# On VectorE, one of four h tiles turned; orders of a two-layer graph kernel made anew; the last z begins as h in three tiles

## What is computed

```python
def reference(x, adj, bias, W_lang, W_grav, W_V, W_O, gate_logit, log_sigma):
    h = layernorm(x + einsum('bnf,nm->bmf', x, adj * adj) + bias)       # layer 0
    z_l, z_g = h @ W_lang.T, h @ W_grav.T                               # layer 1
    v = h @ W_V.T
    zn = z_l / max(norm(z_l), EPS)
    A_l = max(zn @ zn.T, 0) * not_eye
    d2 = max(sq + sq.T - 2 * z_g @ z_g.T, 0)                            # sq = sum(z_g**2)
    A_g = exp(-d2 / (2 * sigma**2)) * not_eye
    K_l, K_g = (A * adj / max(sum(A * adj), EPS) for A in (A_l, A_g))
    K = w * K_l + (1 - w) * K_g                                         # w = sigmoid(gate)
    return layernorm(h + (K @ v) @ W_O.T)
```

## Time and profile before

| | us |
|---|---|
| median of 3 runs | 587.3 (585.48 to 588.52) |
| the profiled execution, timed | 588.2 |
| its span in the profile | 586.2 |

### The profile page before, as it was taken

How to read it: one execution, slowest core, us unless ns; L and a number is a source line. 1 busy time by engine, 2 the same in 40 slices (tenths; PEclk the granted TensorE clock), 3 DMA queues, 4 the chain that set the end, 5 groups by cost and what they waited for, 6 DMA issues and landing times.

```text
span 586.2 us, 9873 instructions
## 1 busy us (share of the span) xinstructions
PE 573.7 (98%) x3653; PEld 445.0 (76%) x3653; DVE 422.2 (72%) x956; ACT 293.5 (50%) x516; POOL 128.0 (22%) x344
## 2 busy tenths in 40 slices
PE   8999999999999999999999999999999999999993
PEld 6887868687786868688686868778686868868771
DVE  4943785858688685858779585868868585877584
ACT  4644536365553546465463636555354646535341
POOL 0201113132222303122221313222230312222021
PEclk9999999999999999999999999999999999999997
DMA  8813031321313031131303112131313110100011
GB/s 273 212 39 72 1 73 32 72 61 55 91 51 76 37 99 29 54 91 56 89 29 98 38 63 65 54 91 44 82 37 94 35 55 18 55 18 22 33 73 72
DMA packets 20783, 38.67 MB, mean 66 GB/s; under 512 B 2176, under 2 KB 2176, under 8 KB 20736
## 3 DMA queue, kind: packets, MB, share of 16 engines
q1 hardware_dynamic: 20736, 38.05, 23.0%
HBM read 21.27 MB, written 16.78 MB: 65 GB/s over the span
## 4 chain that ended last, share of the span: by engine, by line
PE 95%; DVE 2%; DMA 1%; issue 0%; POOL 0%; SPq 0%; ACT 0%; POOLq 0%; DVEq 0%
PE ring L389 65%; PE bank_s L408 10%; PE bank_y L349 3%; PE bank_z L430 3%; PE bank_y L430 2%; PE bank_z L362 2%; PE bank_y L362 2%; PE bank_s L349 2%; PE ring L480 2%; PE ring L503 1%; DMA yT<-in_L_gnn_W_lang_dram 1%; PE bank_s L480 1%; PE bank_y L415 0%; PE bank_s L503 0%; PE ring L473 0%
## 5 line engine op out<-in xcount | busy, mean ns | idle before, releaser
L567 ACT ACTIVATE yT<-ring 128x512 f32<-128x512 f32 x128 | 73.0, 595 | 153.1 <-PE ring L389 153.1
L389 PE MATMUL ring<-hT_hi,T_hi 128*128 128x512 f32 x320 | 126.3, 395 | 0.0
L389 PE MATMUL ring<-hT_hi,T_lo 128*128 128x512 f32 x320 | 124.5, 389 | 0.0
L389 PE MATMUL ring<-hT_lo,T_hi 128*128 128x512 f32 x288 | 112.2, 390 | 0.0
L389 PE MATMUL ring<-M_hi,hT_hi 128*128 128x512 f32 x256 | 102.9, 402 | 0.0
L773 DVE TENSOR_TENSOR hT_lo<-hT,hT_hi 128x512 fp32r<-128x512 f32 x64 | 42.3, 682 | 80.0 <-ACT hT L567 79.6
L389 PE MATMUL ring<-M_lo,hT_hi 128*128 128x512 f32 x256 | 100.0, 390 | 0.0
L389 PE MATMUL ring<-M_hi,hT_lo 128*128 128x512 f32 x256 | 99.9, 390 | 0.0
L389 PEld LDWEIGHTS ring<-hT_hi,T_hi 128*128 128x128 f32 x320 | 60.1, 188 | 25.1 <-issue 12.2
L609 ACT ACTIVATE h_sb<-h_sb,z_nb,z_rs 128x512 f32<-128x512 f32 x62 | 50.3, 813 | 43.2 <-POOL z_nb L1095 43.2
L389 PEld LDWEIGHTS ring<-hT_hi,T_lo 128*128 128x128 f32 x320 | 60.1, 188 | 12.6
(11 more groups left out here) (141 smaller groups left out, 821.3 us busy)
## 6 DMA issues: line engine op xcount, KB each, us to landing
x_sb<-in_x_dram SPq DMA_DIRECT2D x32, 512.0 KB, 6.5
out_dram<-h_sb SPq DMA_DIRECT2D x60, 256.0 KB, 2.0
yT<-in_L_gnn_W_lang_dram SPq DMA_DIRECT2D x4, 256.0 KB, 3.6
yT<-in_L_gnn_W_grav_dram SPq DMA_DIRECT2D x1, 1024.0 KB, 7.3
h_sb<-in_L_gnn_W_V_dram SPq DMA_DIRECT2D x1, 1024.0 KB, 11.8
h_sb<-in_L_gnn_W_O_dram SPq DMA_DIRECT2D x1, 1024.0 KB, 12.7
out_dram<-h_sb SPq DMA_DIRECT2D x8, 128.0 KB, 2.3
bias_bc<-in_L_gnn_bias_dram SPq DMA_DIRECT2D x1, 256.0 KB, 9.0
```

The source lines that it names most:

```text
L389: last = pe.matmul(ring[ring_of(g, k)][:, :], a, b, start=n == 0, stop=n == len(terms) - 1)
L567: return act.activation(dst, src, ACT.Copy, scale=scale)
```

## The change

1. From group 1 on the last of the four h tiles (p = 3) is turned by VectorE, in the new function `turn_h`. Its first instruction turns the 32x32 blocks of the whole tile in place, each in its own 32 partitions, straight from `h_sb` into `hT`; twelve more, of 32 partitions by 128 elements, then write the blocks whose partitions differ. ScalarE makes `hT_hi` of this tile from `hT` in SBUF, and makes no `hT` copy. The new semaphores are `hT_turned_own` and `hT_turned`; `copied` counts the three tiles a group that are still turned by TensorE.
2. The orders of `step` are new on TensorE, ScalarE, VectorE and GpSimd. TensorE does both halves of layer 0, then both of apply_k; one transposed tile goes ahead of the gram, and two behind projection 9.
3. In the last group `residual` is done for tiles 1, 2 and 3, ahead of `apply_k(g, 0)`; tile 1 is counted from PSUM and loses its addition on VectorE.

The core of the diff (of the orders a few lines):

```diff
+            def turn_h(g):
+                dve.wait_ge(h_ready, NP * g + NP)
+                B = N // 2
+                to = hT_view(hT[g % 2], NP - 1).rearrange("f i c (q b) -> f i c q b", q=2)
+                rows_h = h_sb[g % 3][:, NP - 1, :].rearrange("r (i k b) -> r i k b", i=DC, k=4)
+                dve.transpose(hT_view(hT[g % 2], NP - 1),
+                              h_sb[g % 3][:, NP - 1, :].rearrange("r (i c n) -> r i c n", i=DC, c=2)).then_inc(
+                                  hT_turned_own, 1)
+                dve.wait_ge(hT_turned_own, g)
+                for k in range(4):
+                    for q in range(4):
+                        if k != q:
+                            last = dve.transpose(to[k * B:(k + 1) * B, :, q // 2, q % 2, :],
+                                                 rows_h[q * B:(q + 1) * B, :, k, :])
+                last.then_inc(hT_turned, 1)
...
             def hi_hT(g, p):
-                act.wait_ge(hT_done, NP * g + p + 1)
+                if g > 0 and p == NP - 1:
+                    act.wait_ge(hT_turned, g)
+                    copy(hT_view(hT_hi[g % 2], p), hT_view(hT[g % 2], p)).then_inc(hT_hi_done, 1)
+                    return
+                act.wait_ge(hT_done, copied(g, p))
...
@@ TensorE, step
                 layer0(g + 1, 0)
+                layer0(g + 1, 1)
                 if tail:
                     apply_k(g - 1, 0)
-                layer0(g + 1, 1)
-                if tail:
                     apply_k(g - 1, 1)
...
                 transpose_h(g + 1, 0)
-                transpose_h(g + 1, 1)
                 gram(g)
                 project(g, 9)
+                transpose_h(g + 1, 1)
                 transpose_h(g + 1, 2)
-                transpose_h(g + 1, 3)
...
@@ TensorE, last group
-            apply_k(g, 0)
+            residual(g, 1)
             residual(g, 2)
             residual(g, 3)
+            apply_k(g, 0)
             apply_k(g, 1)
...
@@ ScalarE, step
-                evict(g, 6)
                 normalise_h(g + 1, 0)
                 normalise_h(g + 1, 1)
+                normalise_h(g + 1, 2)
+                evict(g, 6)
+                normalise_h(g + 1, 3)
                 evict(g, 7)
...
@@ VectorE, last group
             add_z(g, 0)
-            add_z(g, 1)
+            count_last_z(g, 1)
             count_z(g, 0)
-            count_z(g, 1)
...
@@ GpSimd, step
                 scale_y(g + 1, 0)
+                scale_y(g + 1, 1)
                 if tail:
                     scale_z(g - 1, 0)
-                scale_y(g + 1, 1)
+                    scale_z(g - 1, 1)
                 columns(g)
-                if tail:
-                    scale_z(g - 1, 1)
```

More of the change, by code:

```diff
@@ L196, in bass_two_layer_graph_resnorm @@
         hT_copied = sem("hT_copied")
+        hT_turned_own = sem("hT_turned_own")
+        hT_turned = sem("hT_turned")
         hT_split = sem("hT_split")
@@ L253, in y_bank, with copied @@
             return bank_s if p == 2 else ring[ring_of_y(g)]
+        RES = 1
+        def copied(g, p):
+            return (NP - 1) * g + 1 + min(p + 1, NP - 1) if g > 0 else p + 1
         def z_bank(p):
@@ L345, in layer0 @@
                     pe.wait_ge(hT_split, NP * g - 2)
-                    pe.wait_ge(hT_copied, NP * g - 2)
+                    pe.wait_ge(hT_copied, copied(g - 1, 1))
                 for c in range(2):
@@ L394, in gram @@
                 pe.wait_ge(proj_out, NPROJ * g + 2 * DC)
-                pe.wait_ge(hT_copied, NP * g + NP)
+                pe.wait_ge(hT_copied, copied(g, NP - 1))
                 pe.wait_ge(hT_doubled, g + 1)
@@ L425, in apply_k @@
                 else:
-                    pe.wait_ge(hT_split, NP * g + 2 * NP)
-                    pe.wait_ge(hT_copied, NP * g + 2 * NP)
+                    pe.wait_ge(hT_split, NP * g + 2 * NP - 1)
+                    pe.wait_ge(hT_copied, copied(g + 1, NP - 2))
                 for c in range(2):
@@ L430, in apply_k @@
                         last = pe.matmul(z_bank(2 * h + a)[half(c), :], KT[half(a), h, half(c)], u_sb[half(a), 2 * h + c, :],
-                                         start=g < NG - 1 or h == 0, stop=True, tile_position=(a * N, c * N))
+                                         start=g < NG - 1 or 2 * h + a < RES, stop=True, tile_position=(a * N, c * N))
                 last.then_inc(ku_done, 2)
@@ L607, in normalise_out @@
                 act.wait_ge(z_scale, 2 * g + p // 2 + 1)
-                src = z_bank(p)[:, :] if g == NG - 1 and p >= 2 else h_sb[g % 3][:, p, :]
+                src = z_bank(p)[:, :] if g == NG - 1 and p >= RES else h_sb[g % 3][:, p, :]
                 act.activation(h_sb[g % 3][:, p, :], src, ACT.Identity, scale=z_rs[:, p:p + 1],
@@ L618, in step @@
                 evict(g, 5)
-                evict(g, 6)
                 normalise_h(g + 1, 0)
                 normalise_h(g + 1, 1)
+                normalise_h(g + 1, 2)
+                evict(g, 6)
+                normalise_h(g + 1, 3)
                 evict(g, 7)
+                evict(g, 8)
+                copy_p(g)
                 if tail:
                     normalise_out(g - 1, 0)
-                evict(g, 8)
                 hi_hT(g + 1, 0)
-                hi_hT(g + 1, 1)
-                normalise_h(g + 1, 2)
                 copy_hT(g + 1, 0)
                 copy_hT(g + 1, 1)
-                normalise_h(g + 1, 3)
-                copy_p(g)
+                copy_hT(g + 1, 2)
+                hi_hT(g + 1, 1)
                 hi_hT(g + 1, 2)
-                copy_hT(g + 1, 2)
                 if tail:
                     normalise_out(g - 1, 1)
+                hi_hT(g + 1, 3)
                 evict(g, 9)
-                hi_hT(g + 1, 3)
-                copy_hT(g + 1, 3)
                 if tail:
                     normalise_out(g - 1, 2)
+                    normalise_out(g - 1, 3)
+                exp_g(g)
                 evict(g, 10)
-                exp_g(g)
                 evict(g, 11)
-                if tail:
-                    normalise_out(g - 1, 3)
             def hi_weight(i, c):
@@ L916, in step @@
                 add_y(g + 1, 1)
+                add_y(g + 1, 2)
+                add_y(g + 1, 3)
                 if tail:
                     add_z(g - 1, 0)
-                add_y(g + 1, 2)
+                count_y(g + 1, 0)
                 if tail:
                     add_z(g - 1, 1)
-                add_y(g + 1, 3)
-                count_y(g + 1, 0)
+                count_y(g + 1, 1)
                 if tail:
                     count_z(g - 1, 0)
-                count_y(g + 1, 1)
-                if tail:
                     count_z(g - 1, 1)
                     add_z(g - 1, 2)
-                    gather_z(g - 1, 0)
-                    count_z(g - 1, 2)
-                    add_z(g - 1, 3)
+                    add_z(g - 1, 3)
+                    count_z(g - 1, 2)
+                    count_z(g - 1, 3)
+                turn_h(g + 1)
+                if tail:
+                    gather_z(g - 1, 0)
+                diagonals(g)
+                if tail:
+                    gather_z(g - 1, 1)
+                shift(g)
+                turn_p(g)
                 lo_hT(g + 1, 0)
                 lo_hT(g + 1, 1)
[L935 to L939, removed]
+                add_p(g)
                 lo_hT(g + 1, 2)
-                add_p(g)
-                if tail:
-                    gather_z(g - 1, 1)
                 lo_hT(g + 1, 3)
```

5 lines of the change are left out of this document (2 added, 3 removed).

## The result

The changed kernel takes 579.8 us (median of 4 runs, 579.1 to 580.3) against 587.8 (585.5 to 588.5): a ratio of 0.986, interval 0.984 to 0.989, 8.0 us less. The forecast was 578.7, range 576.8 to 583.0; it was 8.6 less than a median of 587.3, to which the 587.8 here adds the profiled execution (588.2).

A forecast was written before the change was run, and what follows sets the result against it. TensorE, busy 98% of the span, was taken as the bound: 588.2 (profiled run) - 6.5 (steps) - 2.1 (end) = 579.6, or 578.7 us in the runs' terms, range 576.8 to 583.0.

The forecast's parts named there:

- TensorE's saving: Loop steps: one tile of four transposes leaves TensorE from group 1 on, 15 x 0.43 = 6.5 us, bounds 5.3 and 7.4.
- orders give nothing: TensorE's step: layer 0 and apply_k change places, the same sixteen matmuls in another order, saving nothing.
- The walk along VectorE: VectorE's step: turn_h, about 4.55 us, runs 223.5 to 228.1, hidden wholly in the old 5.12 us wait.
- The wait for P_sb: VectorE before diagonals: released at 229.7 by the sooner gram, with 1.4 us still spare after the turn.
- KT was to be ready: Chain to KT in each step: 15.0 us, ready at 244.7, margin 1.0 us before layer 0's second half.
- The last hT_lo: VectorE's last hT_lo subtraction: ends at 237.2, margin 0.9 us before projection 0 of the next group at 238.1.
- The E_g wait: VectorE's chain to KT: its 0.70 us wait for E_g disappears.
- inv_rep: GpSimd, after the second z scale now put ahead: ready near 235.7, needed at 237.2, margin 1.5 us.
- The end: Last group: three residuals before KT at full clock, without the 2.25 us idle; gain 2.1 us, bounds 0.5 and 3.2.
- VectorE becomes the bound: Rival, loop steps: stalls if the twelve turns cost over 0.50 us each, slower from 0.55; 616 at 0.71; chance 0.06.
- Handoffs that eat the margins: Rival, longer relay between engines: TensorE stalls 0.1 to 0.5 us a step, giving 583.2 us; chance 0.14.
- A lone tile as dear as two: Rival, TensorE's transposes: a lone tile pays the same switch as two, no step saving, 585.2 us; chance 0.04.

The follow-up runs named there:

- the added turns: Changed kernel with 4, 8 or 12 more 32x128 turns per step on VectorE into an unread spare buffer: 580.2, 594.7 and 632.2 us.

## Why the prediction was right

**TensorE's saving** was 15 x 0.43 = 6.5. The steps show 6.0 for 14 and 0.45 for the last, 6.5. (The prediction has thirteen other full steps that look alike; they are twelve, and the first, 31.79 us, gains the same 0.43.) That orders give nothing was right too, shown by the kernel with orders and no turn.

**The walk along VectorE.** The start of the turn was worked out as 223.5 on the clock of before. In the trace it is 220.82, and layer 0 stands 2.64 earlier (209.07 against 211.71), so 223.46. The cost was 4.55, measured 225.38 - 220.82 = 4.56. The wait for P_sb: 1.4, measured 1.41. KT was to be ready at 244.7; it was at 242.25 + 2.64 = 244.9, and is needed 0.8 later. The last hT_lo was to end at 237.2; it ended at 234.87 + 2.64 = 237.5, 0.6 ahead of the projection, where I had 0.9. Of these tenths 0.2 is VectorE's addition into S beside GpSimd, 0.88 where it was 0.68 (below). The E_g wait went as foreseen, and inv_rep (233.13 + 2.64 = 235.8, worked out 235.7) was in time.

**The end** was 2.1 in the sum and 2.0 in the traces. But the runs show that this term is two things: 0.3 us of order, and 1.7 us that depends on a clock which does not always fall. The term took one trace's clock for every execution's, and took it off a median, although that trace was of an execution 0.9 above the median. That is the likely part of the sum that was mis-sized: 8.6 forecast, 8.0 measured in the medians, although the traces differ by 6.5 + 2.0 and 0.5 of setup scatter. The 0.6 between is within the interval (6.6 to 9.3 us), so the medians alone do not show it.

**The rivals.** That VectorE becomes the bound: not here, the turns cost 0.30 each. It was priced with 1.4 + 0.9 = 2.3 us of room per step; the added turns show 1.4. The margins behind (0.9 for hT_lo and KT) are not added to the slack ahead in a loop that repeats, because VectorE does the same 31 us of work in every step, and a delay is still there when the next step begins unless a wait takes it up. At 12 turns of 0.50 each, where I put the first stall, the kernel would by this already lose some 0.9 a step. The Trainium skill's rule ("VectorE: DVE Perf Modes", Rules for kernel authors: a 128x128 transpose goes to TensorE if PSUM may take it) names the cheaper engine here too, 0.43 us against 4.56 for four such transposes; as a choice this case disagrees with it, since TensorE was the bound and VectorE was not. By the 390 ns that its section The three transpose paths gives for bf16, the saving was an estimated 1.56 us a step; the steps show 0.43. Handoffs that eat the margins: they took 0.1 to 0.3, and no stall. A lone tile as dear as two: no, 0.53 against 0.97.

## What to carry to other kernels

Work can be moved from the bound engine to one that does it ten times slower, if the other's idle time lies in one piece where the data are ready; the same turn took 6.6 us off the time with the new orders and put 77 us on it in the old ones. In a loop, the room on an engine is the step less its own work less the waits that its order leaves unfilled, and single margins must not be added up; dummy instructions measure it in a few runs. A wait that may or may not bring the half clock is worth filling even with work that is not free, but its worth should be given as two numbers.

## What the runs showed of the hardware

After waits of TensorE of 1.9 to 2.4 us the granted clock falls to its lower level (0.50, 1.2 GHz) in some cases and stays at full in others, in one execution even (the windows above). Of the eighteen such waits in the loops and ends of all these traces it fell behind twelve. It fell behind all fourteen of 3.4 us in the turn in the old orders, and stayed at 1.00 behind the one of 2.90 there. Behind waits of 0.53 to 0.75 it stayed at 1.00 every time.

VectorE and GpSimd lengthen each other in some pairings. In the changed kernel GpSimd's copy to inv_rep overlaps the end of a subtraction for hT_lo and the addition into S on VectorE; the copy takes 0.81, where the earlier trace rows has 0.40, and the addition 0.88 (232.79 above). It is so in all fourteen steps where they overlap, and in the kernel with the new orders and no turn as well. In the kernel before, where the copy lies beside VectorE's small turns of P, it takes 0.40 and the addition 0.68 to 0.69 in every step. In the last group of the changed kernel, where GpSimd is idle then, the addition takes 0.69:

```profile
557.87 0.69 DVE L844 TENSOR_TENSOR S<-P_turned,P_sb 128x512 f32<-128x512 f32 x1
```

Which resource they share was not tried.
